# Moving ScalarE's layers, a sigmoid and VectorE's scaling within the first pass of a vision tower on one core

## What is computed

```python
h = tokens(x)                                    # 32 x 38 x 192
h = h + L0_attn(layernorm(h))                    # scan with 16 states per feature
h = h + L0_ffn(layernorm(h))                     # 8 experts of width 768, top 2 of them per token
h = h + L1_attn(layernorm(h))                    # two mamba scans, forward and backward
h = h + L1_ffn(layernorm(h))                     # 8 experts, top 2

def L0_attn(x):                                  # what the change touches
    a, b, c = -abs(mlp_A(x)), mlp_B(x), mlp_C(x) # mlp: silu(x @ w1 + b1) @ w2 + b2
    delta = sigmoid(mlp_d(x))
    state = (delta * state + (1 - delta) * x * b * dt) * exp(a * dt)   # over 38 tokens
    return sum(state * c) + x * D
```

## Time and profile before

| | us |
|---|---|
| median of 3 runs | 962.56 |
| the runs | 957.51, 962.56, 962.96 |
| the profiled execution | 959.42 |
| its span in the trace | 957.5 |
| TensorE busy | 741.1 (77%) |
| VectorE busy | 573.6 (60%) |
| ScalarE busy | 402.2 (42%) |
| POOL busy | 396.1 (41%) |

### The profile page before, as it was taken

How to read it: one execution, slowest core, us unless ns; L and a number is a source line. 1 busy time by engine, 2 the same in 40 slices (tenths; PEclk the granted TensorE clock), 3 DMA queues, 4 the chain that set the end, 5 groups by cost and what they waited for, 6 DMA issues and landing times. The chain is left out here.

```text
span 957.5 us, 11496 instructions
## 1 busy us (share of the span) xinstructions
PE 741.1 (77%) x3608; PEld 584.0 (61%) x3608; DVE 573.6 (60%) x968; ACT 402.2 (42%) x868; POOL 396.1 (41%) x311
## 2 busy tenths in 40 slices
PE   7877877784667879887999578786779885986756
PEld 5655655553446879777889356555556664764434
DVE  4186978979755613312112587988777787789320
ACT  1548374382215234222445446373617361723110
POOL 1055745855662320331013344544538333734503
PEclk8889899896758999999999789899979998997977
DMA  9469655553684577887776878697588558866221
GB/s 350 131 221 335 211 163 131 149 146 98 172 217 137 165 231 232 236 254 209 227 224 191 204 196 218 175 226 187 143 225 220 150 154 226 225 164 179 79 71 27
DMA packets 84668, 179.51 MB, mean 187 GB/s; under 512 B 12740, under 2 KB 32832, under 8 KB 83840
## 3 DMA queue, kind: packets, MB, share of 16 engines
q1 hardware_dynamic: 79776, 171.55, 63.7%
q0 software_dynamic: 4832, 7.24, 2.6%
HBM read 158.02 MB, written 20.69 MB: 187 GB/s over the span
## 5 line engine op out<-in xcount | busy, mean ns | idle before, releaser
L1665 PE MATMUL PS<-PR,CM 128*128 128x304 f32 (+1 forms) x672 | 186.3, 418 | 84.6 <-POOL PR L790 58.9
L790 POOL TENSOR_TENSOR PR<-ST,V 128x608 f32<-128x608 f32 x96 | 142.2, 1481 | 185.6 <-DVE ST L1299 158.6
L1665 PEld LDWEIGHTS PS<-PR,CM 128*128 128x128 f32 x672 | 124.2, 217 | 129.6 <-POOL PR L790 73.0
L956 ACT ACTIVATE dA<-dA,negA 128x304 f32<-128x304 f32 x192 | 93.6, 538 | 152.2 <-DMA BB<-rows_d 152.0
L1299 DVE TENSOR_TENSOR_SCAN ST<-dA,PS 128x608 f32<-128x608 f32 x96 | 136.3, 1420 | 15.0 <-ACT dA L956 11.0
L1008 ACT ACTIVATE HID<-PS,WX 128x128 f32<-128x128 f32 x204 | 59.6, 367 | 144.1 <-PE PS L1665 144.0
L703 POOL TENSOR_TENSOR dA<-dA,aP 128x607 f32<-128x607 f32 x48 | 71.2, 1484 | 84.6 <-ACT aP L976 82.9
L1495 DVE TENSOR_TENSOR xp<-PS,WXB 128x192 f32<-128x192 f32 x34 | 12.2, 358 | 128.9 <-PE PS L1665 128.9
L1288 DVE TENSOR_TENSOR PS<-BB,PS 128x608 f32<-128x608 f32 x96 | 76.2, 794 | 21.6 <-DMA BB<-rows_d 10.5
L1665 PE MATMUL PS<-XT,WX 128*128 128x128 f32 x408 | 83.2, 287 | 1.0 <-ACT HID L1008 1.0
L1665 PE MATMUL PS<-XT,WXR 128*128 128x128 f32 x408 | 83.0, 287 | 0.0
(11 more groups left out here) (363 smaller groups left out, 1294.9 us busy)
## 6 DMA issues: line engine op xcount, KB each, us to landing
dA<-rows_d SPq DMA_DIRECT2D x144, 304.0 KB, 4.3
BB<-rows_d SPq DMA_DIRECT2D x144, 304.0 KB, 4.7
WX<-ex_m SPq DMA_DIRECT2D x34, 576.0 KB, 4.0
WX<-ex_m SPq DMA_DIRECT2D x34, 387.0 KB, 3.9
slots_d<-WXR SPq DMA_DIRECT2D x8, 960.0 KB, 8.9
WXR<-ex_r SPq DMA_DIRECT2D x34, 192.0 KB, 4.6
WX<-gates_d SPq DMA_DIRECT2D x4, 1216.0 KB, 6.3
CM<-c SPq DMA_DIRECT2D x1, 4430.0 KB, 19.9
```

The lines of the kernel that those rows point to most:

```text
L790: nc.gpsimd.tensor_tensor(PRq[:, c % 2], STq[:, c % 2], DIRS[k].Cw.unsqueeze(1).broadcast_to([128, QB, T]), ALU.mult).then_inc(q_product.s ...
L956: last = nc.scalar.activation(dAq[:, slot, i, :], dAq[:, slot, i, :], ACT.Exp, scale=negA[:, j:j + 1])
L1665: return nc.tensor.matmul(out, lhsT, rhs, start=first, stop=last)
```

## The change

- The 11 layers go in batches of 3, 4 and 4 (steps 2, 3, 4), not of 3, 3, 3 and 2 (steps 2 to 5), at ScalarE and TensorE.
- ScalarE's sigmoid follows the last of them; before it stood ahead of the third batch (in R0 ahead of the second). The copies into p_UP come a step later, and behind the sigmoid.
- VectorE does the routed group's `scale` after scan step 6, not 5, and so `first_scan_input` in R1 to R3.
- The router's logits go to step 7 at TensorE and ScalarE, and `token_rows` stands ahead of `logits_T`.

```diff
@@ ScalarE, first(s, p, m)
                         if n == 2:
                             hidden(p, 0, 3)
-                        if n == (3 if s is None else 4):
+                        if n == 3:
+                            hidden(p, 3, 7)
+                        if n == 4:
+                            hidden(p, 7, 11)
+                            delta(s, p)
+                        if n == (4 if s is None else 5):
                             act.wait_ge(P.ln_x.sem, P.ln_x.after(p, 1))
                             if s is not None:
                                 act.wait_ge(P.w_ready.sem, P.w_ready.after(s, 1))
                             nc.scalar.activation(P.UP[:, 0:T], P.Xm[:, :], ACT.Copy)
...
-                            delta(s, p)
-                        if n == 3:
-                            hidden(p, 3, 6)
-                        if n == 4:
-                            hidden(p, 6, 9)
-                        if n == 5:
-                            hidden(p, 9, 11)
...
-                    if n == 6 and m is not None:
+                    if n == 7 and m is not None:
                         logits(M, m, ROUTE_BANK, None)
@@ VectorE, first(s, p, m)
-                    if n == 5 and m is not None:
+                    if n == 6 and m is not None:
                         scale(M, m, 0)
-                    if n == 5 and p is not None:
+                    if n == (6 if s is not None else 5) and p is not None:
                         first_scan_input(p)
@@ TensorE, first(s, p, m)
                         if n == 3:
-                            hidden(p, 3, 6)
+                            hidden(p, 3, 7)
                         if n == 4:
-                            hidden(p, 6, 9)
-                        if n == 5:
-                            hidden(p, 9, 11)
+                            hidden(p, 7, 11)
...
                     if m is not None:
-                        if n == 6:
+                        if n == 7:
                             pe.wait_ge(s_const[1], 32)
                             pe.wait_ge(s_const[2], 32)
                             logits(M, m, ROUTE_BANK, cm("r_w", 0, 128), cr("r_w", 0, 128))
-                        if n == 7:
-                            logits_T(M, m, ROUTE_BANK)
                             if p is not None:
                                 pe.wait_ge(delta_ready.sem, delta_ready.after(p, 1))
                             token_rows(m, (0, 1))
+                            logits_T(M, m, ROUTE_BANK)
```

## The result

| | before | changed |
|---|---|---|
| median, us | 960.84 (957.51 to 962.96) | 982.0 (981.04 to 984.48, 4 runs) |
| ratio, 95% interval | | 1.0227 [1.0188, 1.0267] |
| span of the profiled execution | 957.5 | 979.2 |
| ScalarE busy | 402.2 | 393.6 |
| ACT_TABLE_LOADs | 62 | 55 |

A forecast was written before the change was run, and what follows sets the result against it. VectorE and its order were taken to set the rounds. Terms 7.0 + 3.0 + 5.8 + 0.6 + 2.2 + 0.9 = 19.5 us on 959.4 gave 978.9, or 982 with the median's offset; forecast 980 us, range 967 to 989.

The forecast's parts named there:

- ScalarE's walk: Step-by-step timing of ScalarE's layers, sigmoid, exponentials and copies; in R2 packed x comes at 146.5, 8.5 us later.
- R2 and R3, +3.5 each: Rounds that scan, prepare and route: VectorE waits for packed x, step 8 ends 3.5 us later, +7.0 together.
- the port +1.0 each: VectorE's scan input meets POOL's queued products at their shared port: 1.0 us in each of R1 to R3, bounds 0 to 3.
- the 3.1 us taken off for step 6 in front: R2 and R3: VectorE runs step 6 before the scan input, which was credited with 3.1 us against the later packed x.
- R1, +5.8 and +1.0: Round scanning group 0 and preparing 1: late packed x and late loads cost 5.8 us, the port 1.0 more.
- the SP queue: R1: row writes 8.3 us later hold up the loads behind them, raising +2.9 at step 8 to +5.8 by the last scan.
- R0, +0.6: Round only preparing group 0: layers end sooner, but rows are written and read later; first scan starts 0.6 us later.
- R4, +2.2: Round scanning group 3 and routing 2: logits at step 7 stand behind the block rows' landing, delaying the block chain 2.2 us.
- R5, +0.9: Round only routing group 3: scaling goes behind the block's copy, costing 1.5 us, of which token rows return 0.5; +0.9.
- (b): Rival, faster: the wait for p_DL vanishes, with packed x there by 140.5 in R2; 942 us, chance 0.07.
- (c): Rival: port costs 3 us in each of R1 to R3 and R1's loads come 2 us later still; 987 us, chance 0.15.

The follow-up runs named there:

- pool_wait: Changed kernel with POOL's decay product of step 7 made to wait for the scan input's first half (p_WV written); 977.91 us, ratio 1.0213.
- vec_back: Changed kernel with VectorE's two moves undone (routed scaling and scan input behind scan 5 again); 974.66 us, ratio 1.0198.
- writes_11: Changed kernel with the SP queue's six writes of the scan input moved from c == 9 to c == 11; 977.25 us, ratio 1.0198.

## Why the prediction was right, and where its sum was not

**ScalarE's walk** held. `p_UP` was to end at 146.5 in R2's old times. It ends at 153.87, and R2 itself is 7.78 us late (its first product with B starts at 117.48, before at 109.70), so at 146.1. Nothing of the seven table loads fewer shows in the time; no run changes them alone.

**R2 and R3, +3.5 each, with the port +1.0 each**: the mechanism was right and the port's term too small. From scan 5 to scan 8 they lose 6.0 and 7.6 us, not 4.5. That all of R2 loses only 4.7 is luck: up to scan 5 it takes 1.4 less, mostly what R1's last scan took more (below). The rows of `p_OM` and `p_WV` cost 2.75 us more in R2 (0.85 and 3.12 against 0.40 and 0.82), near the upper bound of 3, not 1.0. I took one stretched instruction, where three products of POOL were queued, and VectorE waited for all of them. By the Trainium skill (SBUF — State Buffer, Who interferes with whom), a VectorE instruction with two operands in SBUF contends with a POOL instruction that reads SBUF, and the one that comes second is blocked; the trace agrees here, 3.12 us in place of 0.82, and it was the better guide to the size. One size was off without a cost: the scaling, given room up to 140.5, met no POOL and took 0.45 and 0.46, so VectorE stood 7.44 us and not 6. In R3 another 0.9 us is in the gap (8.37). pool_wait adds that such a delay can be passed on but not cancelled while both engines start together, and vec_back that the 3.1 us taken off for step 6 in front were bought with just this: net 0.5 to 1.0 a round, which is within the scatter.

**R1, +5.8 and +1.0**: measured 9.8 from scan 0 to scan 11. To scan 8, 3.9 was forecast and 5.6 measured, again the port. Behind scan 8, 2.9 was forecast for the SP queue and 2.8 measured, and writes_11 takes 3.0 away. But the agreement is partly luck. The writes come 11.7 us later, not 8.3, and the waits for loads add up to 3.15 (1.34, 1.57 and 0.24). Two copies of the tokens' part that took 1.14 and 1.16 before take 0.15 and 0.16, and scan 11 meets a product of POOL (112.83 to 114.31), which the round's last scan did not before:

```profile
112.96 2.62 DVE L1276 TENSOR_TENSOR_SCAN ST<-dA,BB 128x608 f32<-128x608 f32 x1
```

R2 gives these 1.2 us back at once: its first product with B waits 0.40 us for TensorE, before 1.64. Another 1.4 us comes in steps 1 to 5, which I had not looked at; all kernels with the sigmoid last have it (17.8 to 19.9 us against 17.0 to 17.6 in the others), and its cause is open.

**R0, +0.6**: the first scan ends 0.8 sooner. Kernels that share R0's code differ by over 2 us, so neither is shown.

**R4, +2.2, and R5, +0.9**: the step failed, not as a mechanism but as a cost. In R4 the logits do stand behind the landing of the block rows, and the first and second blocks' copies come 1.1 and 1.2 us later in the round (304.26 and 309.30 against 281.06 and 286.02, with the round 22.1 us late), where 0 and 2 were forecast. But R4 ends no later. TensorE, which I had costed at its low clock, is at the high one from the logits' second half on:

```profile
306.05 1.17 PE L1663 MATMUL PS<-m_Xm,CM 128*128 128x304 f32 x2
307.06 0.68 PE L1663 MATMUL PS<-m_Xr,CR 128*128 128x304 f32 x2
```

Before, the layers of the first block still ran at the low one until 289.5. Whether this is what paid for the logits is not shown: R4 takes 80.2 us here and 77.3 in writes_11, with the same code in it. In R5 the blocks' output copies fall back by 1.9 us behind the moved scaling (from 21.86 to 23.74 late) and recover 1.5 of it by 529.04, now 551.27.

**The sum**: 19.5 forecast and 21.7 in the span. R1 to R3 have 23.2 where 15.8 were given (with the port), R0, R4 and R5 together -1.5 (with what follows) where 3.7 were. So the right total is in part luck, by terms that cancel. Of the rivals, (b), faster, fell on the packed x at 146.1 against the 140.5 it needed; (c) had the size of the port right, and with it 987, but not what R0, R4 and R5 left out.

## What to carry to other kernels

Ask of a moved producer not only how late it comes but what its consumer can do meanwhile: with the same late sigmoid the kernel was 2.3% slower when VectorE stood still for it, and no slower than before when the copies came sooner and one more step of the scan lay ahead of it. Look at what the same event releases on the engine that shares a port, and finish the short instructions before the long ones start. And when a gap is filled, the next wait is often one round of a rotating tile or one in-order queue further: three such waits had to be moved in turn before any time was won.

## What was not expected of the hardware

One VectorE instruction can be stretched over two POOL instructions in a row. `p_WV` does not show it yet: its two instructions took 1.58 and 1.62 us beside POOL's 1.62 and 1.70, about one each. But in R4 of the changed kernel one scaling of 128x304 took seven times its usual 0.45, until both of the POOL products beside it were over (294.16 to 295.62 and 295.58 to 297.04):

```profile
294.20 3.17 DVE L1164 TENSOR_TENSOR m_Xm<-q_Cm,q_RS 128x304 f32<-128x304 f32 x1
```

It cost nothing there, since VectorE then waited 6.5 us for TensorE anyway. POOL is stretched too, but little (1.47 to 1.70 beside `p_WV`).
